# Partial sums of softmax weights in two attentions: which tiles go through them, and which engine adds which head

## The reference, cut to what matters

```python
def _mha(x, y, wq, wk, wv, ..., causal):
    xn = _ln(x, lnx_g, lnx_b); yn = _ln(y, lny_g, lny_b)
    q = jnp.einsum('bsc,hcd->bhsd', xn, wq)        # 16 heads of width 32
    k = jnp.einsum('btc,hcd->bhtd', yn, wk)
    v = jnp.einsum('btc,hcd->bhtd', yn, wv)
    a = jax.nn.softmax(jnp.einsum('bhsd,bhtd->bhst', q, k) * D ** (-0.5), axis=-1)
    if causal:                                      # after the softmax
        mask = (jnp.arange(t)[None, :] > jnp.arange(s)[:, None])
        a = a * mask
    o = jnp.einsum('bhst,bhtd->bhsd', a, v)
    ...
```

## Time and profile before

| what | value |
|---|---|
| median of 3 runs | 4138.86 us |
| lowest and highest of the runs | 4130.42 and 4160.15 us |
| the profiled execution, its own time | 4170.53 us |
| span of its trace, first to last instruction | 4168.8 us |
| chunks of `a1` | about 1372 to 2352 us of the span |
| chunks of `a2` | about 2663 to 3462 us of the span |
| mean clock granted to TensorE | 0.899 of full speed |

### The profile page before, as it was taken

The page is one execution under the profiler, slowest core; times in us unless marked ns, Lnnn a source line. Parts: engine busy times, 40 slices in busy tenths (PEclk is TensorE's granted clock), DMA queues, the critical chain, the costliest instruction groups (busy, mean ns, idle before and its releaser), DMA issues. The chain is left out here.

```text
span 4168.8 us, 66056 instructions
## 1 busy us (share of the span) xinstructions
PE 3451.8 (83%) x23063; PEld 1585.2 (38%) x23063; DVE 2533.2 (61%) x4809; ACT 1936.3 (46%) x3897; POOL 1257.1 (30%) x658
## 2 busy tenths in 40 slices
PE   4999999518855999999999773899999994838997
PEld 1333333307752232333322442233333323526775
DVE  4777774481135777687776245777777744344564
ACT  1677777001101456565666361355555561512442
POOL 2000000102211000010000161377777783524454
PEclk7999999758876999999999786899999996968998
DMA  1000000336641000000000061100000001562445
GB/s 59 10 16 10 11 7 3 102 118 208 223 150 38 21 8 16 14 11 19 9 6 4 6 193 50 24 11 21 10 21 9 9 1 54 185 245 82 89 83 116
DMA packets 174222, 236.69 MB, mean 57 GB/s; under 512 B 36499, under 2 KB 148442, under 8 KB 166874
## 3 DMA queue, kind: packets, MB, share of 16 engines
q1 hardware_dynamic: 154858, 207.81, 15.9%
q0 software_dynamic: 19056, 24.88, 3.3%
HBM read 136.16 MB, written 66.82 MB: 49 GB/s over the span
## 5 line engine op out<-in xcount | busy, mean ns | idle before, releaser
L1082 DVE TENSOR_REDUCE a_part_max<-a_wb 128x1 f32<-128x512 f32 (+1 forms) x2048 | 1168.3, 626 | 300.7 <-PE a_wb L1154 291.6
L1034 ACT ACTIVATE a_e<-a_sc 128x512 f32<-128x512 f32 (+1 forms) x1472 | 798.1, 598 | 803.3 <-PE a_sc L1185 800.2
L1154 PE MATMUL a_wb<-a_ks,a_qs 96*128 96x512 f16 (+1 forms) x2048 | 746.2, 372 | 48.4 <-DMA a_qs<-a_stage 28.0
L999 POOL TENSOR_TENSOR a_part_sum<-a_part_sum,a_e 128x2048 f32<-128x2048 f32 x128 | 581.4, 4542 | 141.2 <-ACT a_e L1034 78.0
L1185 PE MATMUL a_sc<-a_qs,a_ks 97*128 97x512 f16 (+1 forms) x1472 | 546.0, 384 | 12.9 <-DMA a_qs<-a_neg_max 8.1
L607 DVE TENSOR_REDUCE xa_part_max<-xa_mx 128x2 f32<-128x802 f32 x512 | 472.1, 986 | 131.3 <-PE xa_mx L711 128.3
L543 ACT ACTIVATE xa_e<-xa_sc 128x512 f32<-128x512 f32 (+1 forms) x832 | 445.6, 596 | 128.0 <-PE xa_sc L698 120.4
L1154 PEld LDWEIGHTS a_wb<-a_ks,a_qs 96*128 96x128 f16 x2048 | 200.0, 98 | 657.3 <-DVE a_part_max L1082 473.3
L992 POOL TENSOR_TENSOR a_em<-a_e,a_later 128x512 f32<-128x512 f32 x64 | 81.1, 1267 | 955.1 <-ACT a_e L1034 944.9
L1208 PE MATMUL a_po<-a_e,a_v 128*32 128x512 f32 (+1 forms) x2432 | 323.9, 605 | 1.8 <-ACT a_dc L1012 1.0
L734 PE MATMUL xa_po<-xa_e,xa_v 128*32 128x256 f32 (+1 forms) x3328 | 269.6, 396 | 7.5 <-ACT xa_oc L593 2.6
(11 more groups left out here) (348 smaller groups left out, 4458.2 us busy)
## 6 DMA issues: line engine op xcount, KB each, us to landing
experts_w_up<-in_we SPq DMA_DIRECT2D x32, 1024.0 KB, 7.1
a_ffn_stage<-in_wm SPq DMA_DIRECT2D x72, 272.0 KB, 3.5
expert_halves<-a_ffn_cut SPq DMA_DIRECT2D x72, 272.0 KB, 3.1
wall<-expert_halves SPq DMA_DIRECT2D x18, 1088.0 KB, 19.4
experts_w_down<-in_we SPq DMA_DIRECT2D x32, 512.0 KB
a_qs<-a_stage SPq DMA_DIRECT2D x384, 32.0 KB, 1.8
moe_xr<-sorted_rows SPq DMA_DIRECT2D x79, 136.5 KB
a_ks<-a_stage SPq DMA_DIRECT2D x336, 32.0 KB, 1.8
```

The costliest lines, as they stand in the source:

```text
L999: pool.tensor_tensor(part_sum[:, :, :], part_sum[:, :, :], e[:, (nkt * n + kt) % ering, :, :], ALU.add).then_inc(part_added, 1)
L1034: act.activation(e[:r, m % ering, j, :], sc[(HG * m + j) % NSC][:r, :], ACT.Exp, scale=scale).then_inc(exp_done, 1)
L1082: dve.tensor_reduce(part_max[:, j, t, k:k + 1], src[:, :mxw], AX.X, ALU.max).then_inc(unit_taken, 1)
L1154: last = pe.matmul(dst[:, :mxw], qs[:STACK, j, n % NQ, P * t:P * t + P], ks[:STACK, g % 2, j, mxs[k]:mxs[k] + mxw], start=True, stop=True)
```

## The change

1. In both attentions, `shared` is now made by a rule, `adds_up`. In `a2` it takes kt 1 to 10, 10 tiles per chunk (8 before). In `a1` it takes, for the first, second and third block of queries, 11, 8 and 4 of the tiles that are not passed, and none for the fourth: 92 tiles in all (none before). These tiles are no longer multiplied with ones; instead `part_sum` is, once per chunk that has shared tiles.
2. Each shared tile is added by two engines: POOL adds the first three heads (1536 wide), DVE the fourth (512 wide), each counting on its own semaphore (`pool_added`, `dve_added`). The first shared tile of a chunk is copied instead of added, and the memset goes. ACT and PE wait for both semaphores where they waited for one.
3. DVE's addition of tile m-1 stands in DVE's order behind the units of step 5 of tile m (`add_up`). To place it, DVE goes through the same loop over tiles and steps as PE (`work_at`); the order of the units is as before.
4. The rows are no longer loaded at the start. Each phase loads the one or two that it needs at its own start: `project_out`, `gelu_ffn`, `gate1`, `ctx_block`, and `layernorm` where it has gains.

```diff
+def row_of(a, n):
+    o, k = ROWS[n]
+    return a["rows"][:, o:o + k].partition_broadcast(P).rearrange("p o n -> p (o n)")
...
-            sp.dma_start(rows[:, :], a["rows"].partition_broadcast(P).rearrange("p o n -> p (o n)")).then_inc(loaded, 16)
             sp.dma_start(x_sb[:, :, :], a["x"].rearrange("o (t p) d -> p (o t) d", p=P)).then_inc(loaded, 16)
-            sp.wait_ge(loaded, 48)
+            sp.wait_ge(loaded, 32)
...
+        if affine is not None:
+            @block.sync
+            def _(sp):
+                for i in range(2):
+                    sp.dma_start(gains[i][:, :], affine[i]).then_inc(gains_loaded, 16)
...
                 dve.wait_ge(var_ready, n)
+                dve.wait_ge(gains_loaded, 32)
...
+    ADD_AT = 5
...
-    shared = [[kt for kt in range(1, nkt - 2) if kt % 4 and own_sum and not causal]
-              for n in range(NC)]
+    def adds_up(n, kt):
+        i = kt - (TPC * (n % NCH) if causal else 0)
+        active = nkt - (kt - i)
+        return own_sum and active > TPC and 0 < i and kt < nkt - 2 and (i % 5 != 0 if causal else True)
+    shared = [[kt for kt in range(nkt) if adds_up(n, kt)] for n in range(NC)]
+    NPH = HG - 1
...
@@ gpsimd
-                if not causal:
-                    pool.memset(part_sum[:, :, :], 0.0).then_inc(part_cleared, 1)
-                    pool.wait_ge(part_cleared, n + 1)
...
                         pool.wait_ge(exp_done, HG * (nkt * n + kt + 1))
+                        tile = e[:, (nkt * n + kt) % ering, :NPH, :]
                         if m:
-                            pool.wait_ge(part_added, m)
-                        pool.tensor_tensor(part_sum[:, :, :], part_sum[:, :, :], e[:, (nkt * n + kt) % ering, :, :],
-                                           ALU.add).then_inc(part_added, 1)
+                            pool.wait_ge(pool_added, m)
+                        if kt == shared[n][0]:
+                            pool.tensor_copy(part_sum[:, :NPH, :], tile).then_inc(pool_added, 1)
+                        else:
+                            pool.tensor_tensor(part_sum[:, :NPH, :], part_sum[:, :NPH, :], tile, ALU.add).then_inc(pool_added, 1)
@@ scalar
-                            act.wait_ge(part_added, nshared[n] + shared[n].index(kt) + 1)
+                            act.wait_ge(pool_added, nshared[n] + shared[n].index(kt) + 1)
+                            act.wait_ge(dve_added, nshared[n] + shared[n].index(kt) + 1)
@@ vector
-            for u in order:
+            def add_up(m):
+                n, kt = m // nkt, m % nkt
+                if kt not in shared[n]:
+                    return
+                i = nshared[n] + shared[n].index(kt)
+                tile = e[:, m % ering, NPH:, :]
+                dve.wait_ge(exp_done, HG * (m + 1))
+                if kt == shared[n][0]:
+                    if n:
+                        dve.wait_ge(pv_done, summed[nkt * n])
+                    dve.tensor_copy(part_sum[:, NPH:, :], tile).then_inc(dve_added, 1)
+                else:
+                    dve.wait_ge(dve_added, i)
+                    dve.tensor_tensor(part_sum[:, NPH:, :], part_sum[:, NPH:, :], tile, ALU.add).then_inc(dve_added, 1)
+
+            for u in before:
+                take(u)
+            for m in range(nkt * NC + 1):
+                for step in range(6):
+                    for u in work_at(m, step):
+                        take(u)
+                    if step == ADD_AT and m >= 1:
+                        add_up(m - 1)
+            for u in after:
                 take(u)
@@ tensor
-                if kt == nkt - 1 and not causal:
-                    pe.wait_ge(part_added, nshared[n + 1])
+                if kt == nkt - 1 and shared[n]:
+                    pe.wait_ge(pool_added, nshared[n + 1])
+                    pe.wait_ge(dve_added, nshared[n + 1])
...
@@ project_out, gelu_ffn, gate1, ctx_block (each: a tile, a semaphore, a load, a wait)
             sp.dma_start(wo[:, :, :], wo_dram).then_inc(w_loaded, 16)
+            sp.dma_start(bias[:, :], bias_dram).then_inc(bias_loaded, 16)
...
+            pool.wait_ge(bias_loaded, 16)
```

More of the change, by code:

```diff
@@ L136, in layernorm @@
         eps = sb("eps", [P, 1])
+        gains = [sb(f"gain{i}", [P, width]) for i in range(2)] if affine is not None else None
+        gains_loaded = sem("gains_loaded")
         tp = ps("tp", [P, 4, CH]) if outs else None
@@ L884, in attention_stacked, with work_at @@
         during.append(work)
+    shares = [1, 1, 1, 1, 1, 1 if own_sum else 0]
+    tile_work = [PASSED_WORK if passed(m // nkt, m % nkt) else TILE_WORK for m in range(nkt * NC + 1)]
+    def work_at(m, step):
+        ahead = (m + LEAD) // nkt
+        window = range(max(nkt * ahead - LEAD, 0), min(nkt * (ahead + 1) - LEAD, nkt * NC + 1))
+        work = during[ahead] if ahead < NC else []
+        in_all = sum(shares) * sum(tile_work[k] for k in window)
+        before_tile = sum(shares) * sum(tile_work[k] for k in range(window.start, m))
+        lo, hi = (-(-len(work) * (before_tile + tile_work[m] * sum(shares[:i])) // in_all) for i in (step, step + 1))
+        return work[lo:hi]
     after = [(u, n) for n in (NC - 2, NC - 1) for u in ("divisors", "divide")]
@@ L900, in attention_stacked @@
         later = sb("later", [P, P]) if causal else None
-        part_sum = sb("part_sum", [P, HG, CH]) if own_sum and not causal else None
+        part_sum = sb("part_sum", [P, HG, CH]) if own_sum else None
         part_max = sb("part_max", [P, HG, TPC, nmx])
@@ L1231, in sum_weights, with some_work @@
                 last.then_inc(pv_done, 1)
+            def some_work(m, step):
+                for u in work_at(m, step):
+                    unit(u)
             for u in before:
@@ L1237, in _ @@
             pe.wait_ge(ones_set, 1)
-            shares = [1, 1, 1, 1, 1, 1 if own_sum else 0]
-            tile_work = [PASSED_WORK if passed(m // nkt, m % nkt) else TILE_WORK for m in range(nkt * NC + 1)]
             for m in range(nkt * NC + 1):
                 n, kt = m // nkt, m % nkt
-                ahead = (m + LEAD) // nkt
-                window = range(max(nkt * ahead - LEAD, 0), min(nkt * (ahead + 1) - LEAD, nkt * NC + 1))
-                work = during[ahead] if ahead < NC else []
-                in_all = sum(shares) * sum(tile_work[k] for k in window)
-                def some_work(step):
-                    before_tile = sum(shares) * sum(tile_work[k] for k in range(window.start, m))
-                    lo, hi = (-(-len(work) * (before_tile + tile_work[m] * sum(shares[:i])) // in_all) for i in (step, step + 1))
-                    for u in work[lo:hi]:
-                        unit(u)
                 if kt == 0 and n < NC:
@@ L1305, in _, with gelu_ffn @@
         def _(pool):
+            pool.wait_ge(bias_loaded, 16)
             for t in range(NT):
                 pool.wait_ge(summed, t + 1)
-                pool.tensor_tensor(dst[:, t, :], dst[:, t, :], bias, ALU.add).then_inc(biased, 1)
-def gelu_ffn(nc, a, name, xt, w2_dram, w3_dram, b2, b3, xo, adds, dst, halved):
+                pool.tensor_tensor(dst[:, t, :], dst[:, t, :], bias[:, :], ALU.add).then_inc(biased, 1)
+def gelu_ffn(nc, a, name, xt, w2_dram, w3_dram, b2, b3_dram, xo, adds, dst, halved):
     ctx, sb, ps, sem = phase(nc, name)
@@ L1375, in _ @@
             pool.wait_ge(based, len(adds))
+            pool.wait_ge(b3_loaded, 16)
             for t in range(NT):
-                pool.tensor_tensor(xo[:, t, :], xo[:, t, :], b3, ALU.add).then_inc(based, 1)
+                pool.tensor_tensor(xo[:, t, :], xo[:, t, :], b3[:, :], ALU.add).then_inc(based, 1)
             for i in range(len(pieces)):
@@ L2482, in program @@
         a["ident"] = ident
-        load_constants(nc, a, cols, rows, ident, ones, x)
+        load_constants(nc, a, cols, ident, ones, x)
         def col(n):
@@ L2487, in col @@
             return cols[:, o:o + k]
-        def row(n):
-            o, k = ROWS[n]
-            return rows[:, o:o + k]
         def scope():
@@ L2610, in _ @@
             sp.dma_start(ct[:, 0, :], a["ctx_t"]).then_inc(loaded, 16)
[L2611 removed]
+            sp.dma_start(bv[:, :], row_of(a, "bv0")).then_inc(loaded, 16)
+            sp.wait_ge(loaded, 32)
 def load_tokens(nc, source, target):
```

57 lines of the change are left out of this document (33 added, 24 removed).

## The result

| what | before | changed |
|---|---|---|
| median | 4136.0 us (5 runs) | 4548.71 us (5 runs, 4542.78 to 4571.81) |
| ratio, 95% interval | | 1.0991 (1.0953 to 1.1029) |
| span of the profiled execution | 4168.8 us | 4570.1 us |
| mean granted clock of PE | 0.899 | 0.856 |

The change costs 413 us, 9.9%. The prediction had +219, slower too, and its range ended at 4450: direction right, size outside the range.

What follows compares the result with a forecast made beforehand. PE was taken to bound the kernel, DVE close and POOL behind. Terms 165 + 3 (a2) + 53 (a1) - 2 (rows) gave plus 219 us: 4390 profiled, 4358 on the median, stated as 4360; range 4130 to 4450.

Steps and rivals of the forecast that it cites:

- What bounds the kernel, what PE loses: Both attentions: PE bounds, DVE close, POOL behind; PE loses 32 us of work in a2, 80 in a1, together 112.
- The price of two-operand instructions beside POOL: Shared tiles: DVE's two-operand addition waits for a whole running POOL operation; 3.45 and 0.55 make 4.0 us against 3.5.
- The rival without mutual exclusion: DVE's f32 addition is not shut out by POOL, stays near 0.7 us; 4027 to 4061 us, chance 0.11.
- The order: Shared tiles: POOL as a rule starts tile k+1 before DVE's addition of tile k, so DVE waits and PE's units stall.
- The two cycles: Between ends of DVE additions: short 4.0 us, long 5.8 us when the fourth score waits for a reduction.
- The sum for `a2`: Plus 6.6 or 15.5 us per chunk, taken as 11.0 times 15 chunks: 165 us, bounds 102 and 235; last chunk plus 3.
- the middle: a2, per chunk: 11.0 us, taken between plus 6.6 (all cycles short) and plus 15.5 (five long, three short).
- The count of units: a2: four units stand ahead of the fourth score in some 5 of 8 tiles, making those cycles long; plus 15.5 per chunk.
- The clock rival: PE falls to 1.2 GHz in the long cycles, a third of the tiles at plus 1.6 us; above 4450, chance 0.08.
- The sum for `a1`: Late masks, shared-tile pace, shut-outs and products with `part_sum`, less PE's savings: plus 53 us, bounds minus 40 and plus 100.
- The memset "goes for nothing": The dropped memset of 1.8 us lay in POOL's idle time, so removing it was booked as neither gain nor cost.
- The rows: Loading rows at their use: minus 4.0 us at the start, 1 us each at two waits; minus 2, from minus 4 to plus 14.

Runs made afterwards that it cites:

- the spaced tiles: Changed kernel, all additions on POOL, a2's eight tiles as before, one-operand spreading; a1 shares only two of three tiles behind the diagonal: 4110.21 us, 0.9957.
- the early place: Changed kernel with DVE's addition behind step 1 instead of step 5, and POOL's addition waiting for DVE's of the same tile: 4288.69 us, 1.0337.
- the run with `a2` alone: Changed kernel with no shared tile in a1, a2 and the rows as changed: 4461.07 us, 1.0785.
- the run that keeps PE's sums: Changed kernel in which PE also does its sums of weights for the shared tiles, which are counted twice: 4563.12 us, 1.1008.
- the kernel that shows it alone: Changed kernel with a2's eight tiles per chunk added on POOL alone, a1 and rows as changed, memset still replaced by a copy: 4310.04 us, 1.0401.

## Why the prediction was off

- **What bounds the kernel, what PE loses:** right. With no such conflict and no late mask (the spaced tiles), a1 shrank by the 40 us that PE had less to do.
- **The price of two-operand instructions beside POOL:** right, and it decides. Shown from both sides (0.68 us with one operand, 0.69 us without POOL, 2.29 with both). The rival without mutual exclusion fell. The Trainium skill's "SBUF — State Buffer", section "Who interferes with whom", is borne out by these means, and it holds one line more that I didn't weigh: copies can run in a mode that takes both ports and can then be shut out too, on this chip reductions never. Both agree with the traces (copy 3.41 and 4.49 us, reduction 0.69).
- **The order:** right. POOL is one tile ahead in 115 of 144 additions of a2. Turned round, and with DVE's addition at the early place, the loss falls from 413 to 145 us.
- **The two cycles:** both exist, but the short one is rare. Of the 120 intervals in the first 15 chunks of a2, 19 are 4.2 us or less, 22 lie between 4.2 and 5.5, 66 at 5.5 to 6.5 and 13 over 6.5. The long one above is 6.0, others 5.8: 1.82 from DVE's end to POOL's start (I had 1.75), 3.44, 0.55.
- **The sum for `a2`: the step that failed.** "The long cycle is put together from parts and shown by no row, so I take the middle, 11.0". The count of units gave 15.5 per chunk, and the traces show 21.0 (19.6 in the run with `a2` alone). Chunk 4: key tile 3 +3.2 us (I had 3.5, but for DVE's first copy; it is the spreading copy), the seven tiles behind it 38.1 instead of 24.0, +14.1, key tiles 11 and 12 +1.9 where I had let 1.0 be made up. The eight intervals of a chunk add up to 44.4 us on average; 5 long and 3 short ones give 41.0, the middle 36.5. So of the 147 us by which a2 was short, 68 (15 times 4.5) are the middle taken against my own count. The other 80 are what the count itself lacked: most of its short cycles were longer than 4.0, some long ones were over 6.5, and arrears grow instead of being made up.
- **The clock rival** (0.08): the clock did fall, to 0.86 in a2, but what it cost is shown by no run (see the run that keeps PE's sums). I had treated it as a case of its own; long cycles, with PE working half of them, were its condition, so the forecast should have carried it.
- **The sum for `a1`:** +84 against +53, within its bounds. The late mask is real: PE waits 38 us for masks in the changed kernel's a1, 6.5 before. What the 31 us beyond my sum are is not taken apart; the spreading copy can be only a small part (at most 1.54 us each in a1). Two terms were rounded (56 times 0.4 is 22, 24 times 1.0 is 24), which changes the sum by 2.
- **The memset "goes for nothing":** wrong by its consequence. It held POOL's phase, in which the spreading copy fell between two additions; 68 us in the kernel that shows it alone. In the changed kernel it stands in the place of the 3.5 us that I had booked for another copy, which is shut out in seven chunks as well; with the additions never shut out, both copies leave a2 61 us above before.
- **The rows:** +17.6 (5 to 29 by the interval), above -2 and around my upper end of 14; not located.
- **The range:** 4450 was cut off where forecast and clock rival meet. With the count's own 15.5 the forecast would have been 4428, and the range would have had to reach well past 4450. My own upper bounds (235, 3, 100, 14) add up to 4491, and that would still have missed: a2's bound of 235 was too low by 60 to 80.

## What to carry to other kernels

Before work is given to an idle engine, list each instruction of its neighbour that reads two SBUF operands or copies from SBUF to SBUF, and take the overlap as serial: here one of 0.69 us became one of 2.29, 224 times, and a copy that the diff doesn't touch went from 0.43 to 3.4. If it can't be avoided, let the engine with the short instruction go first, or give it a form with one operand. When an estimate by counting lies at one end of a range, the count is the forecast, not the middle; and a moved phase is a cost to be looked for in instructions that the diff doesn't touch.

## What the runs showed of the hardware

- A copy of 512 f32 from SBUF to SBUF on DVE, 0.43 us alone, takes 3.41 beside a POOL addition of 3.44 and 4.49 beside one of 4.51. A multiplication of the same size with one operand in SBUF and one in PSUM takes 0.69 beside POOL's addition (3055.44 above, inside POOL's 3054.13 to 3057.57), the same as alone. So does a reduction that reads one SBUF operand and writes 512 columns.
- The wait stands in DVE's duration and not in its idle time, so a busy share of 87% hides that the engine stood still. The mean of a group against its shortest (2.29 against 0.67) gives it away.
- POOL's addition is hardly touched by the meeting: 3.50 us on average against 3.45 where DVE comes first.
- Work that PE does in its waits can be free: with 160 us more of it a2 lasts 1088.2 us, without it 1087.1 and 1108.0. The granted clock there is 0.96 with it, and 0.88 and 0.86 without.
